# A decoder layer on one core: Q, K and cross-attention queries projected feature-major, head pairs read back from DRAM in place of TensorE's turns

## The chip, the cores and the metric

The kernel runs on one core of one Trainium2 chip. A core has a matrix engine (TensorE, PE in the profile), VectorE (DVE), ScalarE (ACT), GpSimd (POOL) and SyncE (SP), which here issues every DMA; 16 DMA engines move the data. The metric is the device time of one execution in microseconds. Three runs of the kernel before took 990.64, 994.16 and 994.91 us.

## The reference, cut to what matters

Two sequences of 1024 tokens and 256 features pass a decoder layer of 16 heads of 16 features; the cross-attention has 77 context tokens, the feed-forward 1024 hidden features.

```python
qkv = x @ w_qkv                                   # q, k, v: heads of D = 16 features
q = q * cos + rotate_half(q) * sin                # RoPE, and the same for k
att = softmax(where(causal, q @ k.T * D ** -0.5, min))
x = layernorm(x + (att @ v) @ w_proj)
q = x @ Wq.T + bq;  k = ctx @ Wk.T + bk;  v = ctx @ Wv.T + bv
x = layernorm(x + softmax(where(mask, q @ k.T / 4, -inf)) @ v @ Wo.T + bo)
h = silu(lin(x, w1)) * lin(x, w2)
h = gelu(lin(h, h1));  h = gelu(lin(h, h2))       # lin(x, w) = (x @ w.T) * s, w ternary
x = layernorm(x + lin(h, w3))
```

## The kernel before, in words

Scores are computed with keys on the partitions. Their softmax needs each query's maximum first, which costs a second product with queries on the partitions, read by DVE. Q and K enter these products as a high and a low part in float32r (hi = rounded, lo = rest), so that one product over 64 rows (four rows of 16: hi, hi, lo and a row block for the maxima) has float32's accuracy. A pair of heads fills the 128 partitions, 64 for each head (`SLOT`). There are eight pairs.

**Projections** (`Q` slots). For each tile of 128 tokens PE multiplies tokens (on the partitions) by `w_qkv` (L584), DVE applies RoPE in three products (L1248 to L1250) and GpSimd adds them into `qk_tok` (L1618). So features lie along the free side, while the scores want them on the partitions.

**Turns.** For each pair `stage_hi` (DVE, L1281) and `stage_lo` (POOL, L1624) lay the hi and lo parts side by side in `stage`, four rounds of four PE transposes turn them (`turn`, L635), and ACT copies each round out of PSUM into `turned`, the tiles q_t and k_t (L1068). In cross-attention `x_stage_hi`, `x_turn` (L774) and two copies do the same for the queries into `qx_t`. Five pairs of `turned` buffers are used in rotation (`QKBUF`).

**Attention** (`S` steps, -20 to 57). `STEPS` lists 48 score steps: group of four heads, chunk of 512 queries, block of 128 keys. In step s PE computes four scores (L684), ACT their exponentials (L1103), POOL the causal cut (L1633), and PE the values of step s - 1 (L701). Between the scores stand up to four maximum products of a later pair (`max_unit`, L649), which DVE reduces (L1298, L1300); a pair's 24 maxima end in `split_max`, a transpose (`rows`, L656) and four small DMAs (`move_rows`, L475) that put them as rows into q_t. Score step 0 waits for the rows of pairs 0 and 1. `pair_base` sets where a pair's work stands. Behind the steps come the norm, and the projection of the cross-attention's queries, tile by tile (`norm_stages`; `project_q`, L751; `q_add`, L1372).

**Cross-attention** (`X` steps, -9 to 9 and the norm). Turn, maxima (`x_max`, L788, L791), rows (`x_rows`, `move_rows` as L498) and, from step 0, scores (L811), exponentials, values (L823). A copy of the maxima on ACT for pair p waits until those of pair p - 2 have been moved by DMA, since there are two buffers of `max_rows`; the transpose for pair p waits for the copy of pair p - 2 while step 0 is not passed.

**Feed-forward.** The first sequence's runs as filler inside the second sequence's slots: `PLAN` gives for each chunk and layer the first and the last slot, and, for layers whose gelu can't stand between exponentials, a slot for a burst of gelus on ACT (L1152). Its weights come through a ring of six tiles from `scratch`, a copy of the weights in DRAM made at the start of the kernel (L526) and read once in whole by DVE, to see whether any weight has low bits (`check_piece`, L533). The second sequence's feed-forward stands at the end (L907 on).

Each engine works through its own program in order and waits on semaphores (`wait`). SP's queue is such a program too: a DMA behind a wait is not issued before the wait is passed.

## Time and profile before

| | |
|---|---|
| median of 3 runs | 994.16 us |
| the profiled execution, and its span | 994.44 us, 992.7 us |
| mean granted clock of TensorE | 0.924 of 2.4 GHz |
| PE busy | 869.8 us (88%) |
| DVE, ACT, POOL busy | 559.3, 376.6, 363.5 us |
| first sequence: projections, then score steps from | 0 to 42 us, 76.6 us |
| first sequence: cross-attention's score steps from | 273.6 us |
| second sequence: projections from | 328.0 us |
| second sequence: cross-attention's score steps from | 735.6 us |
| second sequence's feed-forward, to the end | 829 to 992.7 us |
| DMA | 69.37 MB in 24955 packets |

The busy times are sums over the span; which engine sets the pace changes from stage to stage. The stages' limits from the first start of an instruction of a line are read from the timeline.

### The profile page before, as it was taken

The page shows a single profiled execution, that of the slowest core. Times are in us where ns is not written, and L with a number is a line of the kernel's source. Part 1 is how long each engine was busy: PE and PEld are TensorE (multiplying, and loading weights), DVE is VectorE, ACT ScalarE, POOL GpSimd, SP SyncE. Part 2 cuts the span into 40 slices and gives each one's busy share as a digit, 9 for nine tenths or more (in the row PEclk, how much of TensorE's full clock was granted, in tenths as well). Part 3 has the DMA queues.
Part 4 walks back from the last instruction along what each step waited for, and adds up shares of the span by engine and source line. Part 5 has one row for each costly group of instructions (what it writes and reads, how often), then busy time and mean ns, then how long its engine had stood idle before and what let it go on. Part 6 is the DMA issues. An engine that isn't in the chain of part 4 may idle for free.

```text
span 992.7 us, 13083 instructions
## 1 busy us (share of the span) xinstructions
PE 869.8 (88%) x4466; PEld 553.7 (56%) x4466; DVE 559.3 (56%) x1422; ACT 376.6 (38%) x788; POOL 363.5 (37%) x575
## 2 busy tenths in 40 slices
PE   5879999797889877979999878889889869999997
PEld 2544444335725455645454435468765457888886
DVE  4697888777677654675565654342553476116213
ACT  0315665562453122224555664522343433112210
POOL 4312323546254332052222244252433375335433
PEclk9957999769867898979999989999999999999999
DMA  9909101002002111210101202133211126000000
GB/s 311 323 3 401 45 2 44 23 1 78 4 3 85 48 59 64 86 43 23 44 23 44 85 2 65 42 128 107 65 31 59 71 81 252 1 1 22 1 1 23
DMA packets 24955, 69.37 MB, mean 70 GB/s; under 512 B 4539, under 2 KB 12680, under 8 KB 24712
## 3 DMA queue, kind: packets, MB, share of 16 engines
q1 hardware_dynamic: 24888, 68.50, 20.1%
q8 instruction: 39, 0.64, 0.3%
q14 instruction: 28, 0.23, 0.1%
HBM read 65.87 MB, written 13.63 MB: 80 GB/s over the span
## 4 chain that ended last, share of the span: by engine, by line
PE 73%; DVE 12%; POOL 5%; ACT 5%; issue 3%; DMA 1%; SPq 0%; POOLq 0%; DVEq 0%; ACTq 0%
PE bank L880 13%; PE bank L946 11%; PE bank L684 8%; PE bank L701 7%; PE bank L649 5%; PE bank L635 3%; PE bank L584 3%; PE bank L867 3%; DVE bank L1300 3%; PE bank L928 2%; PE bank L823 2%; DVE max_raw L1298 2%; PE bank L811 2%; ACT prob_s L1103 2%; PE bank L734 1%
## 5 line engine op out<-in xcount | busy, mean ns | idle before, releaser
L1103 ACT ACTIVATE prob_s<-bank 128x512 f32<-128x512 f32 (+3 forms) x384 | 166.4, 494 | 131.3 <-PE bank L684 129.0
L1633 POOL TENSOR_SCALAR_AFFINE_SELECT prob_s<-prob_s 128x128 f32<-128x128 f32 x256 | 83.9, 343 | 178.4 <-ACT prob_s L1103 175.9
L1300 DVE CUSTOM_DVE_ANT_0 bank<-bank,causal_bf 128x128 f32<-128x128 f32 (+3 forms) x256 | 122.4, 511 | 46.0 <-PE bank L649 44.5
L649 PE MATMUL bank<-k_t_s,q_t_s 64*128 64x512 f32 (+3 forms) x384 | 135.6, 461 | 14.4 <-DVE max_raw L1300 11.3
L684 PE MATMUL bank<-q_t_s,k_t_s 64*128 64x512 f32 (+3 forms) x384 | 127.7, 431 | 21.5 <-ACT prob_s L1103 21.0
L684 PEld LDWEIGHTS bank<-q_t_s,k_t_s 64*128 64x128 f32 x384 | 61.5, 200 | 108.5 <-ACT prob_s L1103 64.4
L1298 DVE TENSOR_REDUCE max_raw<-bank 128x1 f32<-128x512 f32 x128 | 82.4, 685 | 51.9 <-PE bank L649 51.9
L880 PE MATMUL bank<-hid_f_hi_s,ring_s 128*128 128x512 f32 x256 | 105.7, 413 | 0.5 <-DVE qk_tok_s L1372 0.5
L880 PE MATMUL bank<-hid_f_lo_s,ring_s 128*128 128x512 f32 x256 | 104.2, 407 | 0.0
L946 PE MATMUL bank<-hid_hi_s,home_s 128*128 128x512 f32 x256 | 99.7, 390 | 0.0
L946 PE MATMUL bank<-hid_lo_s,home_s 128*128 128x512 f32 x256 | 99.7, 390 | 0.0
L701 PE MATMUL bank<-prob_s,v_sb_s 128*32 128x512 f32 (+3 forms) x768 | 88.4, 534 | 8.0 <-POOL prob_s L1633 7.1
L1736 POOL TENSOR_TENSOR hid_lo_s<-act_raw_s,hid_hi_s 128x512 fp32r<-128x512 f32 x48 | 62.0, 1291 | 85.5 <-DVE hid_hi_s L1497 85.5
L1660 POOL TENSOR_TENSOR hid_f_lo_s<-raw_s,hid_f_hi_s 128x512 fp32r<-128x512 f32 x48 | 63.2, 1328 | 73.7 <-DVE hid_f_hi_s L1471 73.6
L649 PEld LDWEIGHTS bank<-k_t_s,q_t_s 64*128 64x128 f32 x384 | 62.2, 204 | 47.5 <-DVE max_raw L1300 23.0
L1497 DVE CAST hid_hi_s<-act_raw_s 128x512 fp32r<-128x512 f32 x48 | 21.3, 443 | 102.7 <-ACT act_raw_s L1232 102.2
L1691 POOL TENSOR_TENSOR prob_s<-prob_s,xmask_t 77x512 f32<-77x512 f32 x32 | 38.3, 1216 | 59.7 <-ACT prob_s L1133 59.7
L1232 ACT ACTIVATE act_raw_s<-bank,scales 128x512 f32<-128x512 f32 x32 | 22.1, 690 | 93.2 <-PE bank L946 93.2
L880 PEld LDWEIGHTS bank<-hid_f_hi_s,ring_s 128*128 128x128 f32 x256 | 49.0, 191 | 14.2 <-issue 3.9
L880 PEld LDWEIGHTS bank<-hid_f_lo_s,ring_s 128*128 128x128 f32 x256 | 48.8, 191 | 11.5 <-issue 2.3
L1321 DVE COPY y_sb_s<-bank 128x512 f32<-128x512 f32 x32 | 22.1, 691 | 58.6 <-PE bank L831 35.1
L946 PEld LDWEIGHTS bank<-hid_hi_s,home_s 128*128 128x128 f32 x256 | 48.1, 188 | 10.1
(156 smaller groups left out, 1523.7 us busy)
## 6 DMA issues: line engine op xcount, KB each, us to landing
ring_s<-scratch SPq DMA_DIRECT2D x44, 512.0 KB, 3.3
home_s<-scratch SPq DMA_DIRECT2D x22, 512.0 KB, 6.1
checked_s<-scratch SPq DMA_DIRECT2D x3, 3584.0 KB, 21.8
x_t_s<-in_x_t SPq DMA_DIRECT2D x2, 1024.0 KB, 5.6
x_tok_s<-in_x SPq DMA_DIRECT2D x2, 1024.0 KB, 5.9
out<-tok SPq DMA_DIRECT2D x16, 128.0 KB, 2.9
q_t_s<-max_rows SPq DMA_DIRECT2D x64, 4.0 KB
qx_t_s<-max_rows SPq DMA_DIRECT2D x64, 4.0 KB
```

The lines of the kernel that those rows point to most:

```text
L649: mm(out[:, 0:k1 - k0], qkt(q, p, 0)[r, P * qt:P * (qt + 1)], qkt(q, p, 1)[r, k0:k1], start=True, stop=True).then_inc(S["max_mm"], 1)
L684: mm(S_BANK[q][j][:, 0:CHUNK - q0], qkt(q, p, 1)[r, P * kb:P * (kb + 1)], qkt(q, p, 0)[r, CHUNK * c + q0:CHUNK * (c + 1)], start=True, sto ...
L701: m = mm(Y[32 * j:32 * (j + 1), q0:CHUNK], v_window(v_sb[q][:, kb], 4 * g + j), prob[q][4 * (s % 2) + j][:, 0:CHUNK - q0], start=kb == 0, ...
L880: o = mm(out[:], view(tile_h(tile[:], k), True), view(hid_f[part][:, k]), start=i == 0, stop=i == last)
L946: o = mm(out[:], weight(tile_h(home[PIECE_H[layer] + m][:], k)), view(src[part][:, k]), start=k + part == 0, stop=(k, part) == (KH - 1, 1))
L1103: act.activation(prob[q][4 * (s % 2) + j][:, 0:n], S_BANK[q][j][:, 0:n], ACT.Exp, scale=SCALE).then_inc(S["exp_done"], 1)
L1298: dve.tensor_reduce(dst, out[:], AXX, ALU.max).then_inc(S["max_red"], 1)
L1300: dve.tensor_tensor_reduce(out=out[:, 0:left], in0=out[:, 0:left], in1=L["causal_bf"][:, CHUNK - left:CHUNK], scale=1.0, scalar=NEG, op0=A ...
L1633: pool.affine_select(out=pr, in_=pr, compare_op=ALU.is_ge, fill=0.0, base=0, pattern=[[1, P]], channel_multiplier=-1).then_inc(S["select_d ...
L1660: pt(hid_f[1][:, m], raw[m][:], hid_f[0][:, m].bitcast(F32), ALU.subtract).then_inc(S["f_lo"], 1)
L1691: pt(pr, pr, L["xmask_t"][0:CTX, CHUNK * (s // NG):CHUNK * (s // NG + 1)], ALU.mult).then_inc(S["xmask_pool"], 1)
L1736: pt(dst[1][:, r % 8], act_raw[n % 3][:], dst[0][:, r % 8].bitcast(F32), ALU.subtract).then_inc(S["act_lo"], 1)
```

## The change

Q and K are projected with `w_qkv` as the stationary side, so that features come out on the partitions, two halves of the heads apart (the host sorts the columns: `halves_apart`). A group is Q or K (g % 2) for a chunk of 512 tokens (g // 2). RoPE becomes four DVE products and two POOL adds of 128 x 512 with tables as large as the tokens (four of 512 KB, instead of two of 64 KB), ACT makes the high part, DVE the low part, and SP writes both to `scratch_qk` in DRAM, eight blocks of 128 x 1024. From there SP reads each pair's 64 partitions per head, for q_t and for k_t. Constant rows come from `fill`, copied into the scratch once. The cross-attention's queries go the same way through `scratch_x`. The context's K still goes through PE transposes.

The projections take 6 slots instead of 13, attention begins at step -15 instead of -20, cross-attention at -7 instead of -9, and `PLAN` is written anew. The copy of the weights to `scratch` moves from the start into steps -15 to -5, one piece of 1 MB a step, and its reading for the check into the steps behind.

```diff
-def stage_step(p):
-    return pair_base(p) - 13
-def turn_step(p, i):
-    return pair_base(p) - 12 + i
+def load_step(p):
+    return max(FIRST_STEP, pair_base(p) - 13) if p >= QKBUF else FIRST_STEP
-FIRST_STEP = stage_step(0)
+FIRST_STEP = max_step(0, 0)
...
+Q_SLOTS = 6
...
-    (0, ("w1", "w2"), ("Q", 2), ("Q", 12), None, None),
-    (0, ("h1",), ("S", -18), ("S", -5), None, ("S", -4)),
-    (0, ("h2",), ("S", 0), ("S", 27), ("S", 29), ("S", 29)),
+    (0, ("w1", "w2"), ("Q", 4), ("S", -8), None, None),
+    (0, ("h1",), ("S", -6), ("S", 8), ("S", 9), ("S", 9)),
+    (0, ("h2",), ("S", 13), ("S", 27), ("S", 28), ("S", 28)),
...
+        def keep_group(q, g):
+            i, c = g % 2, g // 2
+            wait(sp, q, "rope_lo", 2 * (g + 1))
+            ...
+        def load_pair(q, p, c, arrived):
+            for i in range(2):
+                for hh in range(2):
+                    sp.dma_start(qkt(q, p, i)[SLOT * hh:SLOT * (hh + 1), CHUNK * c[0]:CHUNK * c[1]].bitcast(F32),
+                                 a["scratch_qk"][i, :, DH // 2 * (2 * p + hh):DH // 2 * (2 * p + hh + 1), CHUNK * c[0]:CHUNK * c[1]]
+                                 ).then_inc(S[arrived], 16)
+        def first_pairs(q, c):
+            for g in (2 * c, 2 * c + 1):
+                wait(sp, q, f"qk_out{g}", 32)
+            if c == 0:
...
+                for p in range(2):
+                    load_pair(q, p, (0, 1), f"first_in{p}")
+                return
+            for p in range(2):
+                load_pair(q, p, (1, 2), f"pair_in{p}")
+            load_pair(q, 2, (0, 2), "pair_in2")
+            wait(sp, q, "ctx_turn", 2)
+            load_pair(q, 3, (0, 2), "pair_in3")
+            wait(sp, q, "v_mm", NT)
+            load_pair(q, 4, (0, 2), "pair_in4")
+        def projections(q, t):
+            if t < 4:
+                keep_group(q, t)
+            if t == 1:
+                first_pairs(q, 0)
+            if t == 4:
+                first_pairs(q, 1)
+        def load_queries(q):
+            wait(sp, q, "xq_out", 128)
+            wait(sp, q, "score_mm", 4 * LAST)
+            for p in range(NP):
+                for hh in range(2):
+                    h = 2 * p + hh
+                    sp.dma_start(qx_t[q][p][SLOT * hh:SLOT * (hh + 1), :].bitcast(F32),
+                                 a["scratch_x"][:, DH * h:DH * (h + 1), :]).then_inc(S[f"xq_in{p}"], 16)
...
         for s in range(FIRST_STEP, S_END):
             attention(0, s)
+            n = s - FIRST_STEP
+            if n < PIECES // 2:
+                sp.dma_start(a["scratch"][2 * n:2 * n + 2], a["w_ffn"][2 * n:2 * n + 2]).then_inc(L["scratch_in"], 16)
+            n -= PIECES // 2
+            if 0 <= n < PIECES - 1:
+                sp.wait_ge(L["scratch_in"], 16 * (PIECES // 2))
+                sp.dma_start(checked[:, n], a["scratch"][n]).then_inc(L["check_in"], 16)
...
         sp.wait_ge(S["check_op"], PIECES + 3)
         load_tokens(1)
+        load_tables(1)
         load_context(1)
...
+        def project_qk(q, g):
+            ...
+                    m = mm(bank[QK_BANKS[g % 2][half]][:], L["w_qkv"][:, k, cols:cols + P], x_t[q][:, k, CHUNK * c:CHUNK * (c + 1)],
+                           start=k == 0, stop=k == KD - 1)
...
+        def rope_hi(q, g, half):
+            wait(act, q, "rope_add", 2 * g + half + 1)
+            if g >= 2:
+                wait(act, q, f"qk_out{g - 2}", 32)
+            act.activation(qk_hl[q][g % 2][:, 0, half], roped[q][g % 2][:, 2 * half], ACT.Copy).then_inc(S["rope_hi"], 1)
...
+            for i, (x, by) in enumerate(((first, cos_a), (second, sin_a), (second, cos_b), (first, sin_b))):
+                tt(r[:, i], x[:], by, ALU.mult).then_inc(S["rope_mul"], 1)
...
+        def q_parts(q, t):
+            ...
+            tt(out[:, 0], src, L["bias_q"][:].unsqueeze(2).to_broadcast([P, KD, P]), ALU.add).then_inc(S["q_hi"], 1)
+            wait(dve, q, "q_hi", t + 1)
+            for f in range(KD):
+                dve.scalar_tensor_tensor(out=out[:, 1, f], in0=src[:, f], scalar=L["bias_q"][:, f:f + 1], in1=out[:, 0, f].bitcast(F32),
+                                         op0=ALU.add, op1=ALU.subtract).then_inc(S["q_lo"], 1)
```

How the instructions move shows in three places of the built programs. The first is SP's queue in the first sequence, from the last copy of weights to `scratch` on; q_t_63, q_t_65 and q_t_67 are the q tiles of pairs 0, 1 and 2, into which the rows of maxima are moved, and `checked` is the tile of the check. Before:

```order
L526 DMA scratch<-in_w_ffn 16x16384
L475 DMA q_t_s_63<-max_rows 1x8x128 [waits max_mm,turn_evac,rows_evac]
L475 DMA q_t_s_63<-max_rows 1x8x128 x3
L475 DMA q_t_s_65<-max_rows 1x8x128 [waits max_mm,turn_evac,rows_evac]
L475 DMA q_t_s_65<-max_rows 1x8x128 x3
L533 DMA checked_s_157<-scratch 128x7x1024 [waits scratch_in]
```

After:

```order
L609 DMA scratch<-in_w_ffn 16x16384 x6
L541 DMA q_t_s_63<-max_rows 1x8x128 [waits max_mm,rows_evac]
L541 DMA q_t_s_63<-max_rows 1x8x128 x3
L609 DMA scratch<-in_w_ffn 16x16384 x5
L613 DMA checked_s_159<-scratch 128x1024 [waits scratch_in]
L541 DMA q_t_s_65<-max_rows 1x8x128 [waits max_mm,rows_evac]
L541 DMA q_t_s_65<-max_rows 1x8x128 x3
```

The copies now stand among the row moves, and the wait for all of them stands ahead of pair 1's rows instead of behind.

The second place is SP's queue at the first sequence's cross-attention, up to the first move of rows; before, qx_t_131 is pair 0, w_kv_112 a weight of the second sequence's context:

```order
L463 DMA w_kv_s_112<-in_w_k 128x2x256
L463 DMA w_kv_s_112<-in_w_v 128x2x256
L465 DMA bias_kv_s_118<-in_bk 128x256
L465 DMA bias_kv_s_118<-in_bv 128x256
L498 DMA qx_t_s_131<-max_rows 1x8x128 [waits xmax_mm,xturn_evac,xrows_evac]
L498 DMA qx_t_s_131<-max_rows 1x8x128 x3
```

After, with qx_t_133 as pair 0 and qx_t_140 as pair 7, whose read is the last of sixteen:

```order
L531 DMA qx_t_s_140<-scratch_x 64x1x1024 x2
L454 DMA x_t_s_84<-in_x_t 128x2x1024 [waits check_op]
L464 DMA table_s_55<-in_table 128x1024
L464 DMA table_s_56<-in_table 128x1024
L464 DMA table_s_57<-in_table 128x1024
L464 DMA table_s_58<-in_table 128x1024
L458 DMA ctx_t_s_116<-in_ctx_t 128x2x77
L460 DMA w_kv_s_112<-in_w_k 128x2x256
L460 DMA w_kv_s_112<-in_w_v 128x2x256
L572 DMA qx_t_s_133<-max_rows 1x8x128 [waits xmax_mm,xrows_evac]
```

The reads of the queries and the second sequence's tables are new there, and all of them stand ahead of the moves of rows.

The third place is PE in step 11 of the first sequence: scores of pairs 0 and 1 (q_t_63, q_t_65), maxima of pair 4 (k_t_72), one turn of pair 5. Before:

```order
L684 MATMUL bank<-q_t_s_63,k_t_s_64 128x128
L649 MATMUL bank<-k_t_s_72,q_t_s_71 128x512
L635 MATMUL bank<-ident,stage_q_s_59 128x128 x4
L684 MATMUL bank<-q_t_s_65,k_t_s_66 128x128
L649 MATMUL bank<-k_t_s_72,q_t_s_71 128x128
```

After:

```order
L762 MATMUL bank<-q_t_s_63,k_t_s_64 128x128
L727 MATMUL bank<-k_t_s_72,q_t_s_71 128x512
L762 MATMUL bank<-q_t_s_65,k_t_s_66 128x128
L727 MATMUL bank<-k_t_s_72,q_t_s_71 128x128
L762 MATMUL bank<-q_t_s_65,k_t_s_66 128x128
```

Only the turn is gone; the scores and the maxima keep their order.

## Rows read from the trace of the kernel before

**Rows 1.** The page, chain that ended last, by engine.

```profile
PE 73%; DVE 12%; POOL 5%; ACT 5%; issue 3%; DMA 1%; SPq 0%; POOLq 0%; DVEq 0%; ACTq 0%
```

**Rows 2.** Busy us (instructions) of each engine by window, clock, DMA share, GB/s.

```profile
core 0: us, PE busy (x) PEld busy (x) DVE busy (x) ACT busy (x) POOL busy (x), PEclk, DMA share, GB/s
...
76.60:190.00 113.40, 104.97 (x652) 50.14 (x652) 92.81 (x269) 71.18 (x166) 36.49 (x98) 0.94 0.28 107
...
328.00:381.00 53.00, 41.93 (x144) 26.34 (x144) 30.99 (x57) 9.48 (x20) 20.48 (x16) 0.92 0.18 60
381.00:442.00 61.00, 53.74 (x236) 36.55 (x236) 37.30 (x118) 14.41 (x23) 12.89 (x13) 0.89 0.21 70
```

**Rows 3.** Timeline of PE: start, duration, line; turns L635 and L774.

```profile
81.97 1.11 PE L635 MATMUL bank<-ident,stage_k_s 128*128 128x128 f32 x4
...
99.52 0.66 PE L635 MATMUL bank<-ident,stage_q_s 128*128 128x128 f32 x4
100.11 0.50 PE L684 MATMUL bank<-q_t_s,k_t_s 64*128 64x512 f32 x1
...
262.29 1.19 PE L774 MATMUL bank<-ident,stage_q_s 128*128 128x128 f32 x8
```

**Rows 4.** Timeline of PE: score step 0; cross-attention's steps 0 and 3, both sequences.

```profile
76.61 0.73 PE L684 MATMUL bank<-q_t_s,k_t_s 64*128 64x512 f32 x1
...
273.58 0.69 PE L811 MATMUL bank<-qx_t_s,kx_t 64*77 64x512 f32 x4 [0.88 <-DMA qx_t_s<-max_rows]
...
286.23 1.13 PE L811 MATMUL bank<-qx_t_s,kx_t 64*77 64x512 f32 x4
...
735.63 0.46 PE L811 MATMUL bank<-qx_t_s,kx_t 64*77 64x512 f32 x2
...
755.39 0.46 PE L811 MATMUL bank<-qx_t_s,kx_t 64*77 64x512 f32 x2
```

**Rows 5.** Groups of DVE by form: busy us, mean ns, idle before.

```profile
L1248 DVE TENSOR_TENSOR rope_a_s<-bank,cos_t 128x512 f32<-128x512 f32 x16 | 11.0, 688 | 21.2 <-PE bank L584 21.1
...
L1281 DVE CAST stage_k_s<-qk_tok_s 128x512 fp32r<-128x512 f32 x16 | 9.2, 576 | 0.0
...
L1281 DVE CAST stage_q_s<-qk_tok_s 128x512 fp32r<-128x512 f32 x16 | 7.8, 488 | 0.0
```

**Rows 6.** Windows: the copy to scratch (35 to 40), the check's reads (80 to 85).

```profile
35.00:40.00 5.00, 3.87 (x21) 2.98 (x20) 1.82 (x5) 3.34 (x9) 0.36 (x1) 1.00 1.03 341
...
80.00:85.00 5.00, 4.92 (x24) 2.41 (x20) 3.30 (x10) 3.58 (x8) 1.75 (x6) 0.50 1.04 414
```

**Rows 7.** Timeline of SP's queue: start, duration of the issues, count.

```profile
2.34 0.47 SPq L516 DMA_DIRECT2D w_qkv<-in_w_qkv  x1
...
11.90 4.41 SPq L526 DMA_DIRECT2D scratch<-in_w_ffn  x4
...
412.25 2.69 SPq L475 DMA_DIRECT2D q_t_s<-max_rows  x4
```

**Rows 8.** The page, DMA: packets; issues with count, KB, us to landing.

```profile
DMA packets 24955, 69.37 MB, mean 70 GB/s; under 512 B 4539, under 2 KB 12680, under 8 KB 24712
...
x_t_s<-in_x_t SPq DMA_DIRECT2D x2, 1024.0 KB, 5.6
...
q_t_s<-max_rows SPq DMA_DIRECT2D x64, 4.0 KB
```

**Rows 9.** Chain of waits around the burst of gelus: start, us, what.

```profile
566.95 1.28 ACT L1152
568.87 4.38 ACT raw_s L1152 x7
573.27 1.28 ACT L1103
```

**Rows 10.** Timeline of DVE: the last query tile of each sequence.

```profile
247.96 0.42 DVE L1372 TENSOR_TENSOR qk_tok_s<-bank,bias_q 128x256 f32<-128x256 f32 x1 [0.44 <-PE bank L751]
...
696.43 0.42 DVE L1372 TENSOR_TENSOR qk_tok_s<-bank,bias_q 128x256 f32<-128x256 f32 x1 [2.73 <-PE bank L751]
```

More of the change, by code:

```diff
@@ L118 @@
 for _s in range(FIRST_STEP, FINAL_STEP + 1):
-    ROUNDS += [("turn", p, i) for p in range(NP) for i in range(4) if turn_step(p, i) == _s]
     ROUNDS += [("rows", p, 0) for p in range(NP) if rows_step(p) == _s]
@@ L163 @@
 Y_BANK, R_BANK = 6, 7
-QK_BANKS = (2, 3)
+QK_BANKS = ((0, 1), (2, 3))
 V_BANKS = ((4, 5), (6, 7))
@@ L477, in attention @@
         def attention(q, s):
+            for p in range(QKBUF, NP):
+                if load_step(p) == s:
+                    wait(sp, q, "score_mm", 4 * NS * ((p - QKBUF) // 2 + 1))
+                    load_pair(q, p, (0, 2), f"pair_in{p % QKBUF}")
             for p in range(NP):
@@ L485, in attention @@
                 move_rows(q, p)
+            for c in range(NC):
+                if s == norm_step(4 * c + 3) + 4:
+                    keep_queries(q, c)
+            if s == S_END - 1:
+                load_queries(q)
         def cross_attention(q, s):
@@ L559, in _ @@
                 fill_home(2, range(8, 12))
+            if k < len(SLOTS) and SLOTS[k][0] == "Q":
+                projections(1, SLOTS[k][1])
             if k < len(SLOTS) and SLOTS[k][0] == "S":
@@ L764, in norm_products @@
                     project_q(q, t)
-        def x_turn(q, p, i):
-            if i == 0:
-                wait(pe, q, "xstage_lo", p + 1)
-                wait(pe, q, "xstage_hi", p + 1)
-            out = use_round(q, XROUNDS, XROUND_AT, ("turn", p, i), "x")
-            st = stage[q][0][:].bitcast(F32)
-            for j in range(4):
-                t = 4 * i + j
-                m = pe.transpose(out[:, P * j:P * (j + 1)], st[:, 2 * t:2 * t + 2].rearrange("p h a e -> p (h a e)"), ident[:])
-            m.then_inc(S["xround_mm"], 1)
         def x_max(q, p, u):
@@ L1563, in _ @@
         dve.tensor_copy(low_any[:], S_BANK[0][3][0:1, 0:1]).then_inc(S["flag_set"], 1)
-        for s in range(-XSTAGE, XNORM + NT + 4):
+        for s in range(-XMAX, XNORM + NT + 4):
             cross_attention(0, s)
         first_sequence_done(dve)
+        wait(dve, 1, "table_in", 64)
         for k in range(END_SLOT):
@@ L1718, in _ @@
         fill(1)
-        for s in range(-XSTAGE, XNORM + NT + 4):
+        for s in range(-XMAX, XNORM + NT + 4):
             cross_attention(0, s)
@@ L1750, in rope_tables, with halves_apart @@
     sin[:, :half] *= -1
-    return [np.ascontiguousarray(t.reshape(NT, P, DH).transpose(1, 0, 2)) for t in (cos, sin)]
+    tables = [t[:, part].T for part in (slice(0, half), slice(half, DH)) for t in (cos, sin)]
+    return np.stack([np.tile(t, (H, 1)) for t in tables])
+def halves_apart(w):
+    q, k, v = (w[:, D * i:D * (i + 1)] for i in range(3))
+    parts = [t.reshape(D, H, DH)[:, :, half].reshape(D, P) for t in (q, k) for half in (slice(0, DH // 2), slice(DH // 2, DH))]
+    return np.concatenate([*parts, v], axis=1)
 def weight_tiles(g):
```

351 lines of the change are left out of this document (150 added, 201 removed), and 8 rows, old and new, of the table PLAN.

## The prediction, made before the changed kernel was run

> **What bounds the kernel now.** The page's chain of waits first: TensorE makes 73% of it and DMA 1% [rows 1]. Then the windows by stage, because the kernel has stages with different limits. In the steady part of the first sequence (76.6 to 190 us) PE is busy for 105.0 us and DVE for 92.8 of 113.4 us, so two engines are near their limit and either alone gives back only part of what it is relieved of [rows 2]. In the second sequence the feed-forward matmuls of the first fill PE: 41.9 of 53 us while projecting, 53.7 of 61 us up to the first scores [rows 2]. DMA hardly matters behind 50 us. It matters in the change, so I read its rate: 341 GB/s while the feed-forward weights are copied from DRAM to DRAM, 414 GB/s while they are read into SBUF [rows 6].
>
> **What goes.** 64 turns of self-attention and 32 of cross-attention. One turn of four transposes takes 0.59 us at the full clock (start 99.52 to the next start 100.11), up to 1.11 us at the half clock; two turns of cross-attention take 1.19 us [rows 3]. With them go the copies into the stage on DVE, 0.488 + 0.576 us a pair [rows 5], GpSimd's low parts and ACT's evacuations. In steps at or behind 0 of the first sequence stand 20 turns, 3 of them before 88 us: 17 x 0.59 + 3 x 1.11 = 13.4 us of PE. DVE is relieved of only 5 x 1.06 = 5.3 us and is the next limit, so I take -10 us (bounds -5.3, what DVE gives back, and -13.4).
>
> **What comes: traffic.** Four groups of Q and K write 1.5 MB each to DRAM, eight pairs read 1 MB each, per sequence. Every transfer stands in SP's queue. For the first sequence I add up the queue, with MB of 10^6 bytes. Loads up to the scales: 9.2 MB (the tables 2.1 and the fill 3.1 are new); at 400 GB/s and 341 for the fill, with the small rows of weights at half the rate, until 30 us. Groups 0 and 1, 3.1 MB, wait for rope (a product 0.688 us, 4 a group [rows 5]) only until about 29 us, so they follow at once: 38. About 2 us to be seen landed (a lone 1 MB takes 5.6 us, of which 2.6 are its data at 400 GB/s [rows 8]) and the first bytes of the read: first pairs from 41.5 to 46.6. SP waits there in order, so groups 2 and 3 stand behind: 54.5; landed and read from 57.5. No row of before shows a write of 1 MB from SBUF; its rate is bounded by the 341 and 414 GB/s of [rows 6], 3 us in all, and I take 400, as for the loads it resembles.
>
> Now the width of the reads. A pair's read takes from DRAM 8 blocks of 8 rows (L482 of the new kernel), a query's 4 blocks of 16 rows. Do they run on all 16 DMA engines? The page counts 4539 packets under 512 B [rows 8]. 1664 are the short rows of masks (1024), context (512) and scales (128). 2875 are left, and there are 244 issues. If each issue ends with one mark on each engine that it uses, 16 engines for all would make 3904. With 8 for the 128 issues that move 8 short rows of maxima, 11 for the mask of 77 rows and 16 for the other 115, it is 1024 + 11 + 1840 = 2875, to the packet. So an issue is spread over a divisor of its outermost count. For the new reads, whose two sides have different outermost counts (64 partitions against 8 or 4 blocks), no row decides; since a cut has to fall on a block's edge on both sides, I take the smaller: 8 engines for a pair, 4 for queries, 200 and 100 GB/s of the 400.
>
> The Trainium skill states this rule: "DMA: Bandwidth & Descriptors", section "Why a DMA increments its semaphore by 16 and not by 1", lets the slowest dimension of both sides decide, by the largest number up to 16 that divides both. The count of packets agrees with it for equal sides; by it the reads are 8 and 4 wide, and were destinations alone to decide, both would be 16 wide.
>
> Pairs: 4.2 MB at 200 GB/s, 57.5 to 78. Then the copy of 11.5 MB to scratch. Before, it is issued at 11.9 us and hides under the projections [rows 7]; now it is split over steps -15 to -5 and stands behind all that. SP's order, shown with the change, has the wait for the whole copy ahead of pair 1's row moves, without which no score may start, so step 0 waits for the copy. Engine by engine it takes 11.5 MB / 341 GB/s = 34 us, less a little because half the engines start earlier: 110. Then 2.7 us for four row moves [rows 7], 2 to land, 1.5 to be seen: the first score at 116.6 instead of 76.6 [rows 4], +40 us. With full width the pairs take 10.5 us: +30. Bounds: +18 (full width and 414 GB/s throughout), +50 (gaps between the trips twice as long). The maxima no longer count: with step -15 at 46 us they are done by 92.
>
> **Cross-attention of the first sequence.** The last query is added at 248.0 us [rows 10], score step 0 starts 25.6 us later and step 3 at 286.2, 38 us later [rows 4]. Now, from the last query on: hi and lo parts 0.3; the write, 4 issues of 0.47 [rows 7] and 1.6 MB, landed at 6.5; first bytes back at 8; 4.2 MB at 100 GB/s until 49. The next sequence's tokens, tables and context stand between queries and row moves (SP's order). Before, they were long in by then; 3.8 MB more on every engine are 9 us: row 0 lands at 59. ACT copies pair 2's maxima only when pair 0's have been moved, and PE stops at the transpose for pair 4. From there two pairs cost 5 us (2.7 to issue, 2 to land): step 3 at 78 instead of 38, +40 us. With full width the queries are in at 18.5, row 0 at 29.5, step 3 at 48: +10. The 16 turns gone are in neither figure a gain, since PE waits anyway.
>
> **Second sequence up to its queries.** Turns: 32 x 0.59 = -19 us, in PE's own chain here. The trip of Q and K through DRAM leaves PE idle for about 14 us (8 for the context, which stands behind group 3's low part on DVE, 6 for the second half of pair 0); of the idle 11.1 + 7.3 us in those windows before [rows 2] I let 7 go, since the turns' stage is gone: +7. And with twelve fewer slots ahead of step 0 the feed-forward's h1 layer ends only at step 8, so that its gelus come in a second burst on ACT between exponentials: two table loads of 1.28 and 8 gelus, as in the one burst before, from 566.95 to the first exponential behind it at about 574 us [rows 9], in which PE starves: +7. Sum -5, bounds -19 (trip and burst hidden) and +10.
>
> **Cross-attention of the second.** Step 0 stood at 735.6, step 3 at 755.4 [rows 4], 39 and 58 us behind its last query at 697 [rows 10]. The write and read are as above, without tables: row 0 at 50, step 0 at 55.5, step 3 at 76, with feed-forward work between: +18. With full width the turns' 9 us outweigh the trip: -3.
>
> **Small.** Queries get a high and two low parts, 0.5 us more a tile on DVE, 2 us a sequence on the path: +4; pairs 5 and 7 may be read only after scores, 3 steps ahead: +1.
>
> Sum: 40 - 10 + 40 - 5 + 18 + 5 = +88. The profiled execution took 994.4 us (span 992.7), the median is 994.2, so nothing is added: 1082, I say 1080 us.
>
> **Rivals.** (1) The reads run full width: 30 - 10 + 10 - 5 - 3 + 5 = +27, 1021 us. For it: destinations have 64 partitions. Against: the count of packets. (2) Faster: the trips hide. Then the startup must be at most 10 us late, because SP's queue drains before step -4, the turns give all of 13 + 19 + 9 us, and cross-attention loses under 10: about 980 us. It decides where the copy to scratch is done before the maxima of pair 1, that is by 85 us; 31 MB at the highest rate seen, 414 GB/s, are 76 us without any gap, which speaks against it. (3) Nothing changes: gains and trips cancel, 994 us; it needs the same luck in part.
>
> **Numbers.** Narrow reads 0.70, its own range 1045 to 1110 from 20 us of uncertainty in each trip; full width 0.20, 1000 to 1040; faster 0.07; the same 0.03, where within 0.5% is about what can be told from no change. Range 1010 to 1110.
>
> **What would show it.** Right: first score near 117 us, PE idle before it, DMA busy throughout and at half share while pairs are read; 40 us of DMA at a quarter share behind each last query; turns gone, steps of about 2.7 us. Wrong: the first score before 100 us, query reads done in 12 us, or an idle PE in the steady steps.

## The result and the profile after

The changed kernel takes 1143.81 us (median of 4 runs, 1140.22 to 1147.72) against 993.60 us before: the ratio is 1.152, with a 95% interval of 1.147 to 1.156. I had said 1080, with a range of 1010 to 1110. The sign was right, and the time lies outside the range: of 153 us in the profiled execution (span 1145.9 us against 992.7) the sum had 88.

The first view is the length of each stretch. The marks are the starts of PE's instructions in the two traces; "last query" is the last product of the queries' projection. Each column is one execution, and in the first sequence's steps executions of the same program differ by about 3 us: e11, which leaves the first sequence of the kernel before as it is, has 153.7 us there instead of 150.7, and e4 and e10, which leave these steps of the changed kernel as they are, have 163.3 and 162.6 instead of 163.5.

| stretch, us | before | after | change | forecast |
|---|---|---|---|---|
| start to score step 0 | 76.6 | 119.5 | +42.9 | +40 |
| score steps 0 to 47, first sequence | 150.7 | 163.5 | +12.8 | -10 |
| to the last query | 20.2 | 23.5 | +3.3 | small |
| last query to cross-attention's step 3 | 38.7 | 86.2 | +47.5 | +40 |
| to the second sequence's projections | 41.8 | 41.4 | -0.4 | 0 |
| projections to score step 0, second | 115.5 | 98.3 | -17.2 | |
| score steps 0 to 47, second | 213.1 | 243.5 | +30.4 | |
| to the last query | 39.4 | 43.9 | +4.5 | these three: -5 |
| last query to step 3 | 59.4 | 86.5 | +27.1 | +18 |
| to the end | 237.3 | 239.6 | +2.3 | small |

Now the lines that answer to those of before. The page's chain and DMA lines, answering to [rows 1] and [rows 8]:

```profile
PE 56%; SPq 11%; DMA 11%; DVE 9%; ACT 5%; issue 5%; POOL 3%; POOLq 0%; ACTq 0%; DVEq 0%
...
DMA packets 43688, 120.18 MB, mean 105 GB/s; under 512 B 6459, under 2 KB 13960, under 8 KB 43400
```

PE's share of the chain fell from 73% to 56%; SP's queue and DMA, 1% before, are 22%. SP's queue up to the first score, with starts and durations as in [rows 7]:

```profile
40.00 1.35 SPq L481 DMA_DIRECT2D q_t_s<-scratch_qk  x2
...
58.97 1.22 SPq L481 DMA_DIRECT2D q_t_s<-scratch_qk  x2
...
78.32 3.11 SPq L609 DMA_DIRECT2D scratch<-in_w_ffn  x5
115.10 0.34 SPq L613 DMA_DIRECT2D checked_s<-scratch  x1
115.55 2.72 SPq L541 DMA_DIRECT2D q_t_s<-max_rows  x4
```

The last copies are issued by 81.4 us, and then SP stands until 115.1 in the wait for all of the copy; pair 1's rows move right behind it. What PE waited for from 30 us to the first score (us in total, times, longest):

```profile
PE bank L762 <- issue: 24.5, 1, 24.5
PE bank L727 <- DMA k_t_s<-scratch_qk: 18.1, 2, 16.6
PE bank L697 <- DVE ctx_stage_s L1322: 9.8, 1, 9.8
```

"issue" in the first row is time that the profile can't name; by SP's queue it is the wait for rows. The first score starts at 119.51 us [rows 4 had 76.61]. The forecast for that was 116.6, so this step of the prediction held, with its parts: first pairs read from 40.0 (41.5 forecast), the others from 59.0 (57.5).

The windows by stage, columns as in [rows 2]: first the kernel before, from its first score to step 47 in the first and in the second sequence.

```profile
76.60:227.30 150.70, 139.39 (x832) 64.65 (x832) 118.77 (x305) 92.49 (x220) 57.95 (x137) 0.87 0.21 81
...
443.50:656.60 213.10, 191.52 (x1084) 102.47 (x1083) 116.24 (x331) 113.02 (x246) 67.89 (x165) 0.96 0.13 41
```

The same stretches of the changed kernel:

```profile
119.50:283.00 163.50, 145.69 (x760) 65.98 (x760) 116.28 (x293) 83.91 (x200) 52.94 (x131) 0.74 0.31 94
...
532.40:775.90 243.50, 207.57 (x1086) 113.60 (x1085) 117.09 (x327) 115.00 (x240) 71.23 (x164) 0.92 0.20 62
```

Here is what the prediction did not have. In the first sequence 19 turns have gone, 76 transposes (the two traces differ by 72 recorded matmuls), and yet PE is busy for 145.7 us in place of 139.4: the mean granted clock is 0.74 in place of 0.87. By the clock's records, 84 us of the stretch lie at the lower level (1.2 of 2.4 GHz), against 38 before. In the second sequence the count has not changed at all: the turns are gone (76 transposes in this stretch), and 76 more h products of the feed-forward stand in their place, which the new plan has moved behind score step 0.

Cross-attention went as drawn. What PE waited for from the first sequence's last query to step 3 (306 to 393 us):

```profile
PE bank L856 <- DMA qx_t_s<-scratch_x: 26.5, 6, 14.1
PE bank L866 <- ACT max_rows L1127: 22.7, 1, 22.7
```

The first row is the trip, the second the transpose that waits for ACT's copy, which waits for row moves, which stand in SP's queue behind the next sequence's loads:

```profile
313.48 28.13 SPq L531 DMA_DIRECT2D qx_t_s<-scratch_x  x16
341.65 2.30 SPq L454 DMA_DIRECT2D x_t_s<-in_x_t  x1
343.99 11.47 SPq L464 DMA_DIRECT2D table_s<-in_table  x4
...
360.94 2.72 SPq L460 DMA_DIRECT2D w_kv_s<-in_w_v  x1
363.77 27.71 SPq L572 DMA_DIRECT2D qx_t_s<-max_rows  x32
```

While the queries are read, the windows show a quarter of the DMA engines and 105 GB/s (325 to 340 us; the last two columns):

```profile
325.00:340.00 15.00, 8.53 (x37) 7.31 (x36) 6.21 (x16) 0.53 (x2) 0.00 (x0) 0.50 0.26 105
```

That is the forecast's 4 of 16 engines and 100 GB/s.

### The profile page after: what moved, and what is told of

Read it like the earlier page. It is cut to its first block, busy times and chain, and to the rows that moved or that the text cites. A ratio compares the mean times of both kernels' runs of the same rounds, so it can differ in the third digit from the quotient of the medians.

```text
span 1145.9 us, 12423 instructions
## 1 busy us (share of the span) xinstructions
PE 873.8 (76%) x4146; PEld 551.2 (48%) x4146; DVE 555.6 (48%) x1400; ACT 342.8 (30%) x716; POOL 334.2 (29%) x531
## 2 busy tenths in 40 slices
DMA packets 43688, 120.18 MB, mean 105 GB/s; under 512 B 6459, under 2 KB 13960, under 8 KB 43400
## 4 chain that ended last, share of the span: by engine, by line
PE 56%; SPq 11%; DMA 11%; DVE 9%; ACT 5%; issue 5%; POOL 3%; POOLq 0%; ACTq 0%; DVEq 0%
PE bank L948 10%; PE bank L1014 9%; PE bank L762 8%; PE bank L779 7%; SPq L531 5%; PE bank L727 4%; DMA scratch_qk<-qk_hl_s 3%; PE bank L670 2%; DMA q_t_s<-max_rows 2%; ACT prob_s L1162 2%; DMA qx_t_s<-max_rows 2%; PE bank L996 2%; DVE max_raw L1334 2%; PE bank L891 2%; PE bank L935 2%
## 5 line engine op out<-in xcount | busy, mean ns | idle before, releaser
L727 PE MATMUL bank<-k_t_s,q_t_s 64*128 64x512 f32 (+3 forms) x384 | 154.7, 517 | 45.8 <-DMA k_t_s<-scratch_qk 28.0
L762 PE MATMUL bank<-q_t_s,k_t_s 64*128 64x512 f32 (+3 forms) x384 | 139.6, 464 | 60.2 <-ACT prob_s L1162 35.3
L762 PEld LDWEIGHTS bank<-q_t_s,k_t_s 64*128 64x128 f32 x384 | 69.4, 221 | 158.4 <-ACT prob_s L1162 78.9
L727 PEld LDWEIGHTS bank<-k_t_s,q_t_s 64*128 64x128 f32 x384 | 74.6, 233 | 89.0 <-DVE max_raw L1334 34.6
L779 PE MATMUL bank<-prob_s,v_sb_s 128*32 128x512 f32 (+3 forms) x768 | 97.9, 588 | 9.4 <-POOL prob_s L1654 8.8
L1427 DVE TENSOR_REDUCE max_raw<-bank 128x6 f32<-128x462 f32 (+1 forms) x48 | 27.4, 586 | 105.1 <-PE bank L859 105.1
L856 PE MATMUL bank<-xmask_bias,ident_bf 128*128 128x468 bf16 (+1 forms) x48 | 24.9, 518 | 51.9 <-DMA qx_t_s<-scratch_x 51.7
L1127 ACT ACTIVATE max_rows<-bank 32x128 fp32r<-32x128 f32 x32 | 8.4, 264 | 164.7 <-DMA qx_t_s<-max_rows 82.4
```

Source lines behind the costliest of these rows:

```text
L727: mm(out[:, 0:k1 - k0], qkt(q, p, 0)[r, P * qt:P * (qt + 1)], qkt(q, p, 1)[r, k0:k1], start=True, stop=True).then_inc(S["max_mm"], 1)
L762: mm(S_BANK[q][j][:, 0:CHUNK - q0], qkt(q, p, 1)[r, P * kb:P * (kb + 1)], qkt(q, p, 0)[r, CHUNK * c + q0:CHUNK * (c + 1)], start=True, sto ...
L779: m = mm(Y[32 * j:32 * (j + 1), q0:CHUNK], v_window(v_sb[q][:, kb], 4 * g + j), prob[q][4 * (s % 2) + j][:, 0:CHUNK - q0], start=kb == 0, ...
```

## Experiments

Two questions: are the trips and the queue worth what the sum says (e1, e2, e4, e5), and why did the score steps grow where I had them shrink (e3, e7 to e12)? Each ran in 3 rounds beside the kernel before, whose median was 996.9 us beside e1 to e4, 998.0 beside e7, e8, e9 and e11, and 994.9 beside e5, e6, e10 and e12; the ratios are 95% intervals against it. Stretches, as in the table above, of one execution each:

| | median, us | ratio to before | step 0 | steps, first | last query to cross step 0 | projections to step 0, second | steps, second | half clock in the steps, first / second |
|---|---|---|---|---|---|---|---|---|
| before | 993.6 | | 76.6 | 150.7 | 26.1 | 115.5 | 213.1 | 38 / 16 |
| after | 1143.8 | 1.147 to 1.156 | 119.5 | 163.5 | 71.8 | 98.3 | 243.5 | 84 / 41 |
| e1 copy late | 1121.0 | 1.117 to 1.129 | 94.8 | 158.9 | 72.7 | 98.6 | 243.6 | 67 / 41 |
| e2 wide reads | 1082.9 | 1.078 to 1.089 | 116.6 | 160.1 | 43.1 | 95.2 | 243.4 | 77 / 41 |
| e3 dead turns, maxima's bank | 1177.5 | 1.173 to 1.185 | 119.7 | 173.2 | 71.4 | 96.4 | 263.3 | 73 / 51 |
| e4 rows first | 1128.4 | 1.124 to 1.136 | 120.1 | 163.3 | 55.6 | 98.6 | 243.5 | 88 / 41 |
| e5 = e1 + e2 + e4 | 1046.4 | 1.048 to 1.054 | 91.3 | 157.9 | 33.6 | 95.3 | 243.4 | 69 / 41 |
| e7 before, turns doubled | 1009.0 | 1.006 to 1.019 | 79.0 | 154.4 | 24.7 | 123.2 | 213.9 | 36 / 15 |
| e8 dead turns, own bank | 1135.1 | 1.131 to 1.145 | 119.0 | 155.7 | 71.3 | 97.9 | 237.9 | 50 / 20 |
| e9 warm, 84 | 1146.2 | 1.141 to 1.156 | 118.7 | 160.7 | 71.5 | 98.3 | 243.5 | 75 / 41 |
| e10 plan early | 1129.8 | 1.133 to 1.139 | 118.8 | 162.6 | 71.9 | 103.9 | 216.8 | 81 / 27 |
| e11 before, new plan | 1004.0 | 1.003 to 1.008 | 75.9 | 153.7 | 24.8 | 92.9 | 241.7 | 47 / 34 |
| e12 warm, 170 | 1142.0 | 1.144 to 1.150 | 118.5 | 165.3 | 71.9 | 98.4 | 243.4 | 84 / 41 |
| e6 = e5 + e8 + e10 | 1018.4 | 1.021 to 1.027 | 91.0 | 148.6 | 32.6 | 102.1 | 215.0 | 33 / 22 |

**The queue at the start (e1).**

```diff
-            n = s - FIRST_STEP
-            if n < PIECES // 2:
+            n = s - 1
+            if 0 <= n < PIECES // 2:
```

> The changed kernel, with the 11 copies of weights to scratch moved from steps -15..-5 to steps 1..11 and the check's reads behind them (steps 12 to 32). My theory of the startup: SP's queue, with the copy and the wait for it, holds the first score back to 119.5 us. Then it starts near 90 us and the kernel takes about 1115 us (-28). Rival: the maxima and the pairs' reads hold it back, the copy only fills the time; then the first score stays behind 110 us and the time behind 1135.

The first score starts at 94.8 us in place of 119.5, and the kernel is 23 us faster, between the two figures and near the first. The copy was the wait. What is left ahead of the first score is the trip: PE waits 16.5 us for the second half of pair 0, as in the changed kernel (waits of PE, 40 to 95 us, e1):

```profile
PE bank L727 <- DMA k_t_s<-scratch_qk: 16.5, 1, 16.5
PE bank L697 <- DVE ctx_stage_s L1322: 9.0, 1, 9.0
```

**The width of the reads (e2).** The scratch is laid out with the feature row outermost, so that a head's rows are one list of 64.

```diff
-                                 a["scratch_qk"][i, :, DH // 2 * (2 * p + hh):DH // 2 * (2 * p + hh + 1), CHUNK * c[0]:CHUNK * c[1]]
+                                 a["scratch_qk"][i, DH // 2 * (2 * p + hh):DH // 2 * (2 * p + hh + 1), :, CHUNK * c[0]:CHUNK * c[1]].rearrange("p a t -> (p a) t")
...
-                                 a["scratch_x"][:, DH * h:DH * (h + 1), :])
+                                 a["scratch_x"][DH * h:DH * (h + 1)].rearrange("p a t -> (p a) t"))
```

> The changed kernel, with the scratch laid out so that the 64 rows of a head stand behind one another (feature row outermost, block inside); the same bytes, and the reads are one list of 64 rows on both sides. Width theory (an issue runs on as many engines as divide both outermost counts: 8 for pairs, 4 for queries): the queries are read in about 12 us in place of 40, pairs at about 400 GB/s in place of 215; startup -10, cross-attention -28 and -20, about 1088 us. Rival (the reads are slow because of where the rows lie in DRAM or because writes and reads of one tensor disturb each other): the rates stay at 104 and 215 GB/s, time unchanged at 1144.

61 us faster: 28.7 us in the first sequence's cross-attention and 23.3 in the second's, but only 2.9 at the start, where I expected 10. The width is settled by a count too. Packets of e2:

```profile
DMA packets 45433, 120.19 MB, mean 111 GB/s; under 512 B 7484, under 2 KB 14985, under 8 KB 45193
```

The packets under 512 B rise from 6459 to 7484, by 1025. If each issue ends with a mark on each of its engines, 80 issues of pairs going from 8 engines to 16 and 32 issues of queries going from 4 to 16 give 640 + 384 = 1024. But the rate is not the one I expected. While e2 reads its queries:

```profile
315.00:320.00 5.00, 4.45 (x30) 4.09 (x29) 4.70 (x12) 0.53 (x2) 0.00 (x0) 0.82 1.04 229
```

All engines are busy (1.04) at 229 GB/s; a packet of 4 KB takes 0.29 us, against 0.16 us in the changed kernel, where 4 engines make 105 GB/s. Wide reads are 2.2 times as fast, not 4 times, and the forecast's figure for full width, 400 GB/s, was too high. The size of the packets is not the reason: the check's loads into 128 partitions come in packets of 4 KB too and go at 415 GB/s (changed kernel, 139 to 144 us). Whether it is the 64 partitions or the order of the rows in DRAM, no run tells.

**The order of the queue (e4).**

```diff
-        sp.wait_ge(S["check_op"], PIECES + 3)
-        load_tokens(1)
-        load_tables(1)
-        load_context(1)
         for s in range(-XMAX, XLAST):
             cross_attention(0, s)
+        sp.wait_ge(S["check_op"], PIECES + 3)
+        load_tokens(1)
+        load_tables(1)
+        load_context(1)
```

> The changed kernel, with the loads of the second sequence's tokens, tables and context moved from ahead of the cross-attention's row moves of the first sequence to behind them. My theory: rows stand 22 us in SP's queue behind these loads (issued from 341.7 to 363.8), so step 0 of cross-attention comes about 18 us earlier, 1125 us. Rival: row moves are late because the queries' reads are, then under 5 us.

16 us of the stretch, 15 of the kernel. Row moves now start at 341.35 us, when the queries' reads have been issued:

```profile
313.40 27.85 SPq L531 DMA_DIRECT2D qx_t_s<-scratch_x  x16
341.35 28.71 SPq L572 DMA_DIRECT2D qx_t_s<-max_rows  x25
```

**The three together (e5).**

> The changed kernel with the edits of e1 (copy of the weights in steps 1 to 11), e2 (wide reads) and e4 (row moves ahead of the next sequence's loads) together. If they are separate costs in one queue: -23 -61 -15 = 1045 us. Where they overlap (the queue is shared at the start, the rows wait for reads and loads in turn): up to 1060. Rival: a common cause stands behind the three, then no better than the best of them, 1083.

1046.4: the costs add up for the kernel as a whole (-23, -61 and -15 make -99, and it is -97). In the first sequence's cross-attention they don't quite: e2 and e4 take 28.7 and 16.2 us there, the three together 38.4. 51 us over the kernel before are left. The start has 14.7 of them, the score steps 7.2 in the first sequence and 30.3 in the second, against which the stretch ahead of the second's steps is 20.2 us shorter than before.

**Turns as dead work (e3).** Now the steps. Had the turns cost what the forecast took, putting them back must cost that; if they kept the clock up, it must not.

```diff
+            if p >= 2 and u % 6 == 0:
+                for i in range(4):
+                    pe.transpose(out[:, P * i:P * (i + 1)], ident[:], ident[:])
             mm(out[:, 0:k1 - k0], qkt(q, p, 0)[r, P * qt:P * (qt + 1)], qkt(q, p, 1)[r, k0:k1], start=True, stop=True).then_inc(S["max_mm"], 1)
```

> The changed kernel, with four transposes of the identity put back ahead of every sixth maximum product of pairs 2 to 7, into the bank that the product then writes; nothing reads them: as many as before the change (4 turns a pair), 48 turns over both sequences. Clock theory (the score steps run slower than before because TensorE, with the turns gone, is idle more often and is granted half the clock more often): the half clock between the first score and step 47 of the first sequence falls from 84 us towards the 38 us of before, and the time stays or falls, 1125 to 1144 us. Rival 1 (TensorE's time is what counts): 48 x 0.59 = +28 us, 1172. Rival 2 (the steps are slower because of late pair reads and the traffic of the check): no change of the clock, +5 to +28.

34 us slower, and the clock hardly moved: rival 1, it seemed, and my clock theory looked dead. But these turns stand in the bank of the maxima, between DVE's release of the bank and the product that DVE waits for next. The old ones did not. (22 of e3's 24 turns a sequence lie between score steps 0 and 47; before the change it was 19.)

**The same work in its old place (e8).**

```diff
+                if j == 1 and s >= 1 and any(pair_base(p) - 12 + i == s for p in range(NP) for i in range(4)):
+                    last = max(n for n, (kind, i, k) in enumerate(ROUNDS) if (rows_step(i) if kind == "rows" else y_step(i)) < s)
+                    pe.wait_ge(*consumer(q, ROUNDS, last, ""))
+                    for i in range(4):
+                        pe.transpose(R[:, P * i:P * (i + 1)], ident[:], ident[:])
```

> The changed kernel, with four transposes of the identity in each step (from 1 on) in which a turn stood before, into the bank of the turns and at their place behind the second score; nothing reads them. In e3 the dead turns stood in the bank of the maxima, between DVE's reduction and the next product, and cost 0.40 us each in the first sequence and 0.83 in the second. If turns are paid in full wherever they stand: the same again, +25 to +30 us. If they lie in slack: 0 to +8. Clock theory: half clock in the first sequence's score steps falls from 84 us, and the steps take under 163.5 us.

With useless transposes added, the kernel gets faster: 1135.1 us, 1133.4 to 1135.4 in its four runs, where the changed kernel has 1140.2 to 1147.7 and e9, in the same rounds as e8, 1142.8 to 1147.4. From score step 0 to step 47, in both sequences:

```profile
119.00:274.70 155.70, 143.01 (x830) 67.67 (x830) 115.64 (x293) 84.39 (x200) 51.49 (x129) 0.84 0.32 99
524.20:762.10 237.90, 208.92 (x1160) 117.19 (x1159) 116.93 (x327) 114.74 (x240) 71.00 (x164) 0.96 0.21 63
```

70 recorded matmuls more than in the changed kernel (18 dead turns are 72), and PE is busy for 2.7 us less in the first sequence, with a clock of 0.84 in place of 0.74; half clock falls from 84 to 50 us, and in the second sequence from 41 to 20. The other 5.1 us of the 7.8 gained there are idle time of PE; its waits for DVE's reductions fall from 6.1 to 1.4 us (16 and 5 times):

```profile
PE bank L727 <- DVE max_raw L1334: 6.1, 16, 0.6
```

```profile
PE bank L727 <- DVE max_raw L1339: 1.4, 5, 0.4
```

The rival named ahead of e3, late reads of the pairs, is small: PE waits 1.7 us for them in the changed kernel's steps and 1.8 in e8, and the DMA traffic is the same in both (share 0.31 and 0.32). And 21 of the 34 us of half clock that went stood right behind the first score: there it lasts to 149.2 us in the changed kernel and to 128.0 in e8, 30 and 9 us behind the first score (11 in the kernel before, 9 in e6). For e3 the same rows read:

```profile
119.70:292.90 173.20, 157.27 (x848) 73.81 (x848) 115.83 (x293) 85.89 (x200) 52.55 (x129) 0.79 0.29 89
539.70:803.00 263.30, 228.98 (x1176) 126.37 (x1175) 116.83 (x327) 116.77 (x240) 71.38 (x164) 0.90 0.19 57
```

Four dead turns more than in e8, and 17.5 and 25.4 us longer, which four turns of 0.59 or even 1.11 us can't make. So it is the place that decides: between DVE and PE a turn of dead work costs 0.4 to 0.9 us (9.7 and 19.8 us for 22), beside that chain less than nothing. That the clock is the way by which it helps is read from the two clock figures; no run changes the clock alone.

**What a turn cost in the kernel before (e7).**

```diff
-                m = pe.transpose(out[:, P * j:P * (j + 1)], st[:, 2 * t:2 * t + 2].rearrange("p h a e -> p (h a e)"), ident[:])
+                for _ in range(2):
+                    m = pe.transpose(out[:, P * j:P * (j + 1)], st[:, 2 * t:2 * t + 2].rearrange("p h a e -> p (h a e)"), ident[:])
```

> The kernel before, with every transpose of self-attention's turns issued twice (64 turns more, same place and bank, same result). It prices a turn where it stood. TensorE theory (my forecast's price of 0.59 us a turn): about +32 in the second sequence and +10 in the first, 1036 us. Rival (the turns lie in TensorE's slack, so that nothing was to be gained by removing them): under +10 us, most of all in the score steps of the first sequence (150.7 us before).

Neither: +11 us for 64 turns, 0.17 each, not 0.59 (the interval is 6 to 19 us, 0.1 to 0.3 each). By the profiled executions, 7.7 us lie in the stretch ahead of the second sequence's step 0, where 13 turns stand (0.59 each, the full price), but only 3.7 in the first sequence's steps and 0.8 in the second's, with 19 turns each; 3.7 is hardly more than the 3 us by which e11 differs there without an edit. In the score steps, then, most of what a turn takes was free. The profile doesn't show that as idle time: PE's idle time in the first sequence's steps is 11.3 us before and 12.2 in e7. It shows in the order of the starts. One turn and the two maximum products behind it, in the kernel before:

```profile
102.74 0.66 PE L635 MATMUL bank<-ident,stage_k_s 128*128 128x128 f32 x4
...
103.39 0.44 PE L649 MATMUL bank<-k_t_s,q_t_s 64*128 64x384 f32 x1
...
103.99 0.44 PE L649 MATMUL bank<-k_t_s,q_t_s 64*128 64x384 f32 x1
104.35 1.07 PE L701 MATMUL bank<-prob_s,v_sb_s 128*32 128x512 f32 x8
```

The same place in e7:

```profile
105.86 1.09 PE L636 MATMUL bank<-ident,stage_k_s 128*128 128x128 f32 x8
...
106.88 0.44 PE L650 MATMUL bank<-k_t_s,q_t_s 64*128 64x384 f32 x1
...
107.22 0.33 PE L650 MATMUL bank<-k_t_s,q_t_s 64*128 64x384 f32 x1
107.49 1.06 PE L702 MATMUL bank<-prob_s,v_sb_s 128*32 128x512 f32 x8
```

The doubled turn delays the first product by 0.37 us, but the second follows after 0.34 instead of 0.60 us, and the values start 1.63 us behind the turn instead of 1.61. In the kernel before, the second product had waited for DVE, which reduces the two products ahead of these until 103.94 us:

```profile
102.65 1.29 DVE L1298 TENSOR_REDUCE max_raw<-bank 128x1 f32<-128x512 f32 x2 [0.97 <-PE bank L649]
```

In e7 DVE is through with the same two at 107.05 us, ahead of the second product. So the second half of the doubled turn takes the place of a wait, and that wait was counted as busy, since a score product ran beside it (103.67 to 104.06 us).

**The plan (e11, e10).** In e11 the kernel before gets the new table:

```diff
-    (0, ("w1", "w2"), ("Q", 2), ("Q", 12), None, None),
-    (0, ("h1",), ("S", -18), ("S", -5), None, ("S", -4)),
-    (0, ("h2",), ("S", 0), ("S", 27), ("S", 29), ("S", 29)),
+    (0, ("w1", "w2"), ("Q", 4), ("S", -8), None, None),
+    (0, ("h1",), ("S", -6), ("S", 8), ("S", 9), ("S", 9)),
+    (0, ("h2",), ("S", 13), ("S", 27), ("S", 28), ("S", 28)),
...
```

> The kernel before, with the changed kernel's PLAN for the feed-forward (76 h1 products move behind the second sequence's score step 0, with a burst of gelus at step 9). It prices the plan alone. If the plan is what makes the second sequence's score steps 243.5 us long in place of 213.1: they grow by about 31 (76 x 0.41) + 7 for the burst, and the stretch ahead of them shrinks by at most 20, since no turns are gone there: about +18 us. Rival (the steps are slow for lack of clock and late reads): under +8 us in all.

+10 us against the kernel before's profiled execution, +6 by the medians of the same rounds (1004.0 against 998.0), so the price was smaller than expected and, as a sum, in the rival's range of under 8. Stretch by stretch it is the plan's theory that holds: the steps grow by 28.6 us, almost all that the changed kernel shows (30.4), and the stretch ahead of them shrinks by 22.6. In e10 the changed kernel gets an earlier plan:

```diff
-    (0, ("w1", "w2"), ("Q", 4), ("S", -8), None, None),
-    (0, ("h1",), ("S", -6), ("S", 8), ("S", 9), ("S", 9)),
-    (0, ("h2",), ("S", 13), ("S", 27), ("S", 28), ("S", 28)),
+    (0, ("w1", "w2"), ("Q", 2), ("S", -12), None, None),
+    (0, ("h1",), ("S", -11), ("S", -3), None, ("S", -2)),
+    (0, ("h2",), ("S", 2), ("S", 27), ("S", 28), ("S", 28)),
```

> The changed kernel, with the feed-forward's w1, w2 from slot Q 2 to S -12, h1 from S -11 to S -3 (gelus without a burst) and h2 from S 2: the h1 products return ahead of the second sequence's score step 0, where TensorE is idle 20 us. Plan theory: the stretch ahead of step 0 grows by less than 20, the score steps shrink by about 31 + 7: -10 to -18 us, 1130. Rival (the order is worth nothing, total work counts): 1144.

As expected: -14 us by the medians, the stretch ahead +5.6, the steps -26.7 (the profiled executions are 19 us apart, since that of the changed kernel is the slowest of its four). The work went into time in which PE had been idle:

```profile
433.20:537.10 103.90, 88.77 (x334) 58.03 (x335) 67.74 (x163) 23.60 (x40) 26.26 (x20) 0.94 0.55 183
537.10:753.90 216.80, 187.54 (x1012) 98.25 (x1012) 114.99 (x327) 104.62 (x225) 66.97 (x161) 0.94 0.19 55
```

The changed kernel had 30.2 of 36.0 and 48.1 of 62.4 us busy there, at a clock of 0.83 and 0.81.

**Keeping the clock up ahead of step 0 (e9, e12).** In both, dead transposes run in the wait for pair 1's rows, 84 and 170 of them:

```diff
+            if q == 0 and s == 0:
+                for i in range(84):
+                    pe.transpose(S_BANK[0][0][:, P * (i % 4):P * (i % 4 + 1)], ident[:], ident[:])
```

> The changed kernel, with 84 transposes of the identity ahead of the first sequence's first score, in the 22 us in which TensorE waits for rows; nothing reads them. Clock theory: the 30 us of half clock behind the first score (119.5 to 149) come from the idle time before it; they go, and the score steps take about 155 us in place of 163.5: 1136 us. Rival (the steps are slow because of the check's reads and late pairs): steps unchanged, 1144 us, or later by what the transposes overrun the wait.

> As e9, with 170 dead transposes in place of 84: there they ran in 12 us, at the full clock after 98 us, and 13 us of idle followed, with half clock to 142.6. Now TensorE is busy up to about the first score. Clock theory: full clock from the first score on, score steps about 154 us in place of 163.5, 1135 us. Rival (a late start of the steps has other causes than the clock): 161 us or more, 1144 and up.

Both missed. The steps take 160.7 and 165.3 us (the profiled execution of e12 is the slowest of its five; the median is 1142.0). In e12 the transposes end 4.5 us ahead of the first score:

```profile
93.56 20.41 PE L1052 MATMUL bank<-ident 128*128 128x128 f32 x170
118.49 0.76 PE L762 MATMUL bank<-q_t_s,k_t_s 64*128 64x512 f32 x1 [4.53 <-issue]
```

The records have full clock from 96.9 to 117.4 us, and then half clock for 30.7 us, while PE is busy for 9.65 of 10 us and more. Whether these 4.5 us of idle brought it down, or something else did, the runs don't tell: dead work that reaches up to the first score without a gap was not tried. But e8 bears on these 30 us of half clock at the start of the steps: dead turns inside the steps, from step 1 on, cut them to 9, where dead work ahead of the steps leaves 24 (e9) and 30 (e12), and dead turns in the bank of the maxima 29 (e3). So of the places tried, only dead turns in their own bank behind the first score shorten them. They are not the only thing that can: in e1, without any dead work, the half clock ends 9 us behind the first score too, but comes back for 10 us (107.0 to 117.2 us). Why, no run shows.

**All that helped (e6).**

> The edits of e5, e8 (dead turns in their own bank) and e10 (plan) together: 1045 - 9 - 12 = about 1025 us, if each cause is a cost of its own. Not faster than before in any case: the startup (first score about 90 in place of 76.6) and the trips are still there.

1018.4 us, a ratio of 1.021 to 1.027: 125 us faster than the changed kernel, still not as fast as the one before. The steps now take 148.6 and 215.0 us, as before the change (150.7, 213.1); what remains is the late first score (+14.4 us) and some 21 us in all in the norms, the queries' trips and cross-attention, against 13.4 us gained ahead of the second sequence's steps. No version beat the kernel before.

## Why the prediction was wrong

**Held.** The startup (+42.9 for +40), and in it the wait for the copy, which e1 shows; the width of the reads, 8 and 4 engines, by share, rate and e2's count of marks; cross-attention's two waits (+47.5 for +40), of which e2 takes 29 us and e4 16. My rival 1 had a wrong price: full width gives these reads 229 GB/s and not 400, and the kernel with it takes 1083 us (e2), not 1021. Of these 62 us the start and the two trips make 26 (+40.0, +18.8 and +3.8 for +30, +10 and -3); the rest is what follows here.

**Failed: "I take -10 us (bounds -5.3, what DVE gives back, and -13.4)", the turns in the first sequence's steps.** It was +12.8. (It stood on 20 turns at or behind step 0; by `pair_base` there are 19.) Two errors stand in it. First, a turn was priced by the time from its start to the next start, 0.59 us. But in e7 a turn costs 0.2 us or less in the steps (3.7 us for 19 turns, 0.8 for 19). Work outside the chain from PE over DVE's maxima and back is mostly hidden there, and e3 shows what the same transposes cost when they stand in that chain. That PE was busy for 105 of 113 us [rows 2] was true and did not mean that PE set the pace. Second, both bounds had the same sign. With the turns gone, 46 us more of the stretch lie at the half clock; e8 puts useless ones back at their place, and 34 us of half clock and 7.8 us of time go again. The remaining 5 us against before, with 12 us more of half clock, no run takes apart; 3 of them are within what two executions of the kernel before differ by. Nothing in [rows 2] excluded a loss: the column of the clock stood there, 0.94, and I had used its two levels only to price a turn.

**Failed: "Sum -5", the second sequence up to its queries.** It was +17.7. The -19 for the turns is the same error: 13 turns ahead of step 0 are worth 7.7 us (e7), the 19 behind it next to nothing (0.8 us), so 8.5 in place of 19. The +7 for the burst of gelus missed that the new plan moves 76 h products into the steps as well. In the kernel before, that costs 6 us over steps and stretch ahead (e11), but in the changed one, where PE has idle time ahead of the steps, another plan wins 14 us by the medians and 21 by these stretches (e10: +5.6 - 26.7). And the +7 for the trip was too small: e11's 92.9 us ahead of step 0, less 7.7 for the turns, would be 85, and it is 98.3, so the trip, with whatever else the new projections change, costs about 13 us there. This is a difference of executions; no run prices the trip alone. PE's wait for ACT's exponentials in the steps grew from 20.6 to 34.9 us (443 to 656 us before, 532 to 776 after); the plan alone makes it 27.6 (e11), so it is half of the growth:

```profile
PE bank L684 <- ACT prob_s L1103: 20.6, 24, 7.4
```

```profile
PE bank L762 <- ACT prob_s L1162: 34.9, 42, 7.7
```

**Mis-sized: cross-attention,** +47.5 for +40 and +27 for +18. In the first sequence pair 0's rows were to land 59 us behind the last query. Their move is issued at 57.3, but ACT's copy of pair 2, which waits for them, comes at 67.8 (374.28 us); from there to step 3 it is 18.4 us, as forecast (19). In the second sequence the trip is as drawn, with 25.2 us of waits for the reads and 12.8 for the rows, but PE is at half clock for 48 us of it (825 to 839 and 849 to 883 us), so that the work between the waits takes longer. Both are read from the trace; no run takes them apart.

The two failed steps make 46 of the 65 us that were missing, cross-attention's sizes 17 (7.5 and 9), the startup 3. The range had a term of 20 us for each trip and none for a loss in the score steps.

## What to carry to other kernels

Price an instruction that is to be removed by doubling it where it stands: it shows in one run whether it is in the pacing chain or in slack, which a busy share of 93% does not. On this kernel dead work in slack inside the steps went with more full clock and less time, and dead work ahead of them did not; bound the gain of removing such work on the side of a loss too. And where one queue issues all transfers, read the order of that queue before their sizes: the wait for a copy and the loads ahead of the row moves cost 23 and 15 us without being work for any engine.

## What the hardware showed that I had not expected

Reads from DRAM into 64 partitions in packets of 4 KB: on 4 engines each packet takes 0.16 us (105 GB/s), on 16 engines 0.29 us (229 GB/s), while loads of 128 partitions reach 414 GB/s [rows 6]. Useless transposes on TensorE, 72 in each sequence's score steps, went with a kernel that was 9 us faster, and in the first sequence's steps with a mean granted clock of 0.84 in place of 0.74. And after 20.4 us of uninterrupted transposes, the last 17 of them at the full clock, and 4.5 us of idle, the clock was at the half for the next 30.7 us (e12), although TensorE was busy for nearly all of them.
